# Graph aggregation as products of exact bfloat16 parts, with earlier gathers and a new order of attention's turns

## The chip, the core and the metric

One core of a Trainium2 chip runs the whole program: TensorE (PE in the profile; PEld is its weight loads), VectorE (DVE), ScalarE (ACT), GpSimd (POOL) and SyncE (SP, which only issues transfers). The engines run side by side and meet at semaphores. The metric is the device time of one execution in microseconds; before the change the median of three runs is 892.15 us (891.47 to 894.31).

## The reference, cut to what matters

`x` is 1250 rows of 512 float32 numbers; a graph of 20000 edges is given by `src` and `dst`. Two layers follow one another, each a graph step and a mixture of experts:

```python
x = x + _L0_gnn_ref(_layernorm(x), ..., edge_index, W)   # attention along the edges, 8 heads
x = x + _L0_ffn_ref(_layernorm(x)[None], ...)[0]         # 8 experts, the best 2 for each row
x = x + _L1_gnn_ref(_layernorm(x), W, b, gamma, beta, src, dst)
x = x + _L1_ffn_ref(...)                                  # 6 experts, the best 1
```

The third is the one whose arithmetic changes:

```python
h = x * rsqrt(deg_out)[:, None]
agg = segment_sum(h[src], dst)          # sum over incoming edges
h = agg * rsqrt(deg_in)[:, None]
h = layernorm(h @ W + b, gamma, beta)
return gelu(h)
```

The kernel makes `agg` as a dense product: (1250 x 1250 matrix of edge counts) times (1250 x 512 rows h).

## The kernel before

Rows are worked in T = 10 tiles of P = 125; the 512 features are C = 4 chunks of 128. Every engine has its program written out by hand, in order; each instruction waits in its engine's queue for the semaphores it names. There is no scheduler.

**Counts (0 to 178 us).** Edge lists become matrices of counts and of logarithms, stored to DRAM as `counts_d` and `logs_d` (float32), while PE also projects q, k and v. This runs inside a branch (`all_hold`), which the inputs here take; the other arm is for graphs of another kind.

**Attention (178 to 500 us).** 40 units u, four for each row tile, two heads each. In one unit PE does `scores(u+1)` for two thirds of the columns, `turn_output(u-2)` (L731, the turned output of an older unit), `turn_weights(u)` (L704, 20 transposes in 5 blocks of 4, each block moved out of PSUM by ACT, or by DVE for blocks 2 and 4), every fourth unit `turn_normed_row` (L749), then the last third of the scores (L693) and `weigh_values(u-1)` (L722). DVE subtracts logs and keeps minima (L1935), moves blocks (L1942), adds outputs to X. Beside it, tile by tile, runs the routing for the first experts: DVE finishes a tile's statistics in unit 5+4i, POOL makes its root (`rstd_tile`, L1512 and L1513), PE makes logits in unit 7+4i, DVE picks two experts, POOL makes the masks (`masks_of`, L1523), and PE ranks them in unit 8+4i (L766). POOL scatters rows into `slots0_d` by their ranks.

**First experts (500 to 649 us).** MT0 = 27 tiles of 128 slots go through three products (L802) with transposes between (L809), two norms and two GELUs, in a software pipeline. POOL makes two roots a tile (`inverse_rms`, L1573). DVE moves a tile's result to SBUF (`move_made`, L2147), SP stores it back to `slots0_d` (`store_rows0`, L440). Not all 27 tiles hold rows: the inputs here fill 24, and the others lie behind them.

**Gather and aggregate (649 to 736 us).** When every tile is stored, POOL gathers each row's two results (`gather_rows`, L1606, two indirect transfers a tile of rows), DVE adds them to X (`add_rows`, L2216), takes statistics (`row_stats`, L1741), POOL makes a root times the out-degree's (`row_root`), DVE scales the row (`rows_over_root`, L2223) into `HS[i]`, and PE multiplies `HS[i]` with the tile's counts (`aggregate`, L932): 2 pieces of 500 columns by 4 chunks, accumulated over the 10 tiles in all 8 PSUM banks. Gathers are issued AHEAD = 3 tiles ahead: gather i stands behind the root of tile i-2 in POOL's queue. While PE waits for the first rows it runs products whose result nobody reads (`keep_busy`, L924). The last 250 columns (`aggregate_rest`) need free banks and come later.

**Projection and second routing (736 to 818 us).** PE alternates `project` (L959), the four `aggregate_rest` and the routing products; DVE does bias, layer norm, GELU's input, best expert and slot of each tile; POOL scatters the tiles (L1654). **Second experts (818 to 891 us).** 15 tiles, the same way.

Of the kernel before, what the change touches and what calls it, by code (L numbers as in the profile page):

```python
# [8 lines left out]
I32 = mybir.dt.int32  # L9
# [28 lines left out]
FAR = 1.0e28  # L38
TM = 128
# [3 lines left out]
BUSY_AHEAD, BUSY_BETWEEN = 44, 12  # L43
E0, H0, K0 = 8, 256, 2
MT0 = (K0 * N + E0 * (TM - 1)) // TM
E1, H1 = 6, 256
# [48 lines left out]
def gnn_moe_kernel(nc, x, src, dst, L0_gnn_W, L0_ffn_gate_w, L0_ffn_w1, L0_ffn_w2, L0_ffn_w3,  # L95
                   L0_ffn_n1, L0_ffn_n2, L1_gnn_W, L1_gnn_b, L1_gnn_gamma, L1_gnn_beta,
                   L1_ffn_w_gating, L1_ffn_gamma, L1_ffn_w1, L1_ffn_w2, out):
    counts_d = nc.dram_tensor("counts_d", (N, N), F32).ap()
    logs_d = nc.dram_tensor("logs_d", (N, N), F32).ap()
# [3 lines left out]
    with ExitStack() as ctx:  # L103
# [51 lines left out]
        def ring(off, width, n):  # L155
# [12 lines left out]
        CS_C = R_B[0:P, 10000:10000 + (T - 2 * C) * N].rearrange("p (i n) -> p i n", i=T - 2 * C)  # L168
        counts_of = [part[:, i, :] for part, n in ((CS_A, C), (CS_B, C), (CS_C, T - 2 * C)) for i in range(n)]
        HS = [R_B[0:P, 12544 + D * i:12544 + D * i + D] for i in range(T)]  # L170
        BIAS, GAMMA, BETA = (R_B[:, 6144 + 512 * k:6656 + 512 * k] for k in range(3))
        AGT = R_A[:, 0:C * N].rearrange("p (c n) -> p c n", c=C)
        HG = [R_B[0:P, 18688 + D * k:18688 + D * k + D] for k in range(3)] + [R_B[0:P, 8192:8192 + D]]
# [6 lines left out]
        rows = [R_A[0:P, WIDE * n:WIDE * n + WIDE] if n < 12 else R_B[0:P, WIDE * (n - 12):WIDE * (n - 12) + WIDE]  # L180
                for n in range(K0 * T)]
# [3 lines left out]
        count_rows = [R_B[0:P, 14308 + N * k:14308 + N * k + N] for k in range(5)]  # L185
        ident = sb("ident", [128, 128])
# [39 lines left out]
        ssum = sb("ssum", [128, LANES])  # L226
        rms = sb("rms", [128, LANES])
# [6 lines left out]
        def small_bank(b, n):  # L234
# [23 lines left out]
        names = """x_in edges_in w_in wq_in wg_in consts zero_made zeros_out idx_step halves_made idx_turned  # L258
            span_step diag_made span_sums ctl_sums ctl_ready win_made hot slots_free gen_win gen_hot
            gen_free gen_step packed_out unpacked_out ct_made ln_made ln_masked ct_turned ct_moved  # L260
# [6 lines left out]
            y_made y_moved y_out0 y_out1 y_out2 counts_in0 counts_in1 counts_in2 logs_out0 logs_out1  # L267
            vec_in hs_made agg_made agt_moved hg_made hg_biased hg_stat hg_rstd hg_shift hg_gelu gate_sums
            xg_made w1b_in w2b_in gam_in log1_made g1_step g1_exp rank1_made deg_out_made log1_taken
            mask1_made slot1_ready rank1_taken token_made x_kept gate1_made slot1_made rows1_out  # L270
# [16 lines left out]
        y_out = [s["y_out0"], s["y_out1"], s["y_out2"]]  # L287
# [12 lines left out]
        def _(sp):  # L300
# [57 lines left out]
            def load_counts_of(tiles):  # L358
                for i in tiles:
                    if i > 4:  # L360
                        sp.wait_ge(S("deg_out_made"), i - 4)
                    move(count_rows[i % 5], counts_d[i * P:i * P + P, :], count_rows_in[i % 5])
            load_counts_of(range(5))
            for i in range(2, 5):
                load_logs(i)
            load_counts_of((5, 6))
            load_logs(5)
            load_counts_of((7, 8))
            load_logs(6)
            load_counts_of((9,))  # L370
            load_logs(7)
            load_logs(8)
            sp.wait_ge(S("deg_out_made"), T)
            for e in range(E0):
                sp.dma_start(W3E[:, e, :].rearrange("p (c n) -> p c n", c=2),
                             L0_ffn_w3[e].rearrange("(c p) n -> p c n", c=2)).then_inc(S("w3e_in"), 16)
# [51 lines left out]
            def load_counts(i):  # L428

                if i == 0:  # L430
# [2085 lines left out]
```

## Time and profile before

| | us |
|---|---|
| median of three runs | 892.15 |
| profiled execution, its own time | 892.8 |
| its span in the profile | 891.1 |
| PE busy | 839.9 |
| DVE busy | 556.9 |
| ACT busy | 374.2 |
| POOL busy | 207.2 |

The span is what the profile's clock covers; the time of the same execution is 1.7 us longer. A busy PE is not a PE at its peak: the ends of matmuls are modelled. The mean granted clock of TensorE is 0.984 of full speed. An engine's idle time costs only where another engine waits for it.

### The profile page before, as it was taken

What the parts mean: (1) busy time and instruction counts of PE and PEld (TensorE: products, weight loads), DVE (VectorE), ACT (ScalarE), POOL (GpSimd) and SP (SyncE); (2) the same over time, 40 slices, a digit from 0 to 9 for tenths busy, and PEclk for the clock granted to TensorE, in tenths of its full rate; (3) what the DMA queues carried; (4) which work ended last, traced back from release to release, by engine and by line L of the source; (5) the groups of instructions that cost most, each with busy time, mean ns of one, the idle gap of its engine ahead of it and who ended that gap; (6) DMA issues with size and microseconds to landing.
All of it is one profiled execution on the core that took longest, in us unless ns stands there. A gap on an engine that the chain in (4) does not pass through costs nothing.

```text
span 891.1 us, 16170 instructions
## 1 busy us (share of the span) xinstructions
PE 839.9 (94%) x5189; PEld 569.9 (64%) x5189; DVE 556.9 (62%) x1838; ACT 374.2 (42%) x680; POOL 207.2 (23%) x380
## 2 busy tenths in 40 slices
PE   5999999899999999999999899999979999996996
PEld 2456554367777777777777677777664445675664
DVE  6489999267778788778777265555533514875111
ACT  1234544366565566666566233334300012543331
POOL 4200000000022112201202332212245511465353
PEclk9999999999999999999999999999999999996999
DMA  9818888795111232110925546544136250175550
GB/s 261 324 29 220 220 209 210 171 322 137 31 49 57 57 101 61 44 39 25 306 78 156 200 115 212 160 155 154 48 95 138 69 189 12 36 258 136 155 170 22
DMA packets 87362, 121.00 MB, mean 136 GB/s; under 512 B 40781, under 2 KB 50157, under 8 KB 87021
## 3 DMA queue, kind: packets, MB, share of 16 engines
q1 hardware_dynamic: 73677, 101.82, 38.9%
q0 software_dynamic: 13600, 18.11, 7.3%
q8 instruction: 46, 0.75, 0.4%
q14 instruction: 39, 0.32, 0.1%
HBM read 65.52 MB, written 57.08 MB: 138 GB/s over the span
## 4 chain that ended last, share of the span: by engine, by line
PE 76%; DVE 11%; DMA 5%; issue 3%; ACT 2%; POOL 1%; SPq 1%; DVEq 0%; POOLq 0%; ACTq 0%
PE ps L802 18%; PE ps L693 11%; PE ps L722 10%; PE ps L932 10%; PE ps L704 8%; PE ps L583 5%; PE ps L959 4%; PE ps L809 4%; DVE R_B L1834 3%; PE ps L588 2%; DVE R_B L1833 2%; DMA R_A<-slots_d 1%; DVE R_A L1935 1%; PE ps L524 1%; PE ps L759 1%
## 5 line engine op out<-in xcount | busy, mean ns | idle before, releaser
L802 PE MATMUL ps<-R_B,R_A 128*128 x612 | 185.2, 445 | 1.7 <-ACT R_A L1302 0.6
L802 PEld LDWEIGHTS ps<-R_B,R_A 128*128 128x128 f32 x612 | 111.6, 193 | 34.6 <-issue 24.5
L1238 ACT ACTIVATE R_A<-R_A,neg_max 125x1250 f32<-125x1250 f32 x80 | 106.6, 1333 | 56.9 <-DVE neg_max L1935 56.9
L1935 DVE CUSTOM_DVE_ANT_0 R_A<-ps,R_B,neg_max 125x417 f32<-125x417 f32 (+1 forms) x160 | 97.6, 648 | 29.1 <-PE ps L693 29.1
L693 PE MATMUL ps<-R_B 64*125 64x417 f32 (+1 forms) x480 | 106.5, 544 | 1.9 <-ACT XN L1180 1.5
L722 PEld LDWEIGHTS ps<-R_W,XN 125*64 125x64 f32 x1600 | 85.3, 136 | 23.1 <-issue 23.0
L704 PE MATMUL ps<-ident,R_A 125*125 125x125 f32 x800 | 98.7, 278 | 0.0
L704 PEld LDWEIGHTS ps<-ident,R_A 125*125 125x125 f32 x800 | 94.9, 188 | 1.5 <-DVE R_W L1942 0.7
L722 PE MATMUL ps<-R_W,XN 125*64 125x125 f32 x1600 | 94.7, 272 | 0.0
L1245 ACT ACTIVATE R_W<-ps 125x500 f32<-125x500 f32 x120 | 66.1, 585 | 51.4 <-PE ps L704 51.4
L583 PE MATMUL ps<-XT,R_W 128*128 128x500 f32 (+1 forms) x192 | 72.5, 523 | 0.6 <-ACT XT L1163 0.6
L1935 DVE CUSTOM_DVE_ANT_0 R_A<-ps,R_B 125x417 f32<-125x417 f32 x80 | 44.1, 590 | 45.1 <-PE ps L693 32.4
L1834 DVE TENSOR_SCALAR R_B<-R_B 125x418 bf16<-125x418 uint16 x180 | 69.0, 383 | 0.0
L809 PEld LDWEIGHTS ps<-ident,R_A 128*128 128x128 f32 x306 | 38.3, 142 | 34.5 <-issue 20.0
L693 PEld LDWEIGHTS ps<-R_B 64*125 64x125 f32 x480 | 39.7, 183 | 29.4 <-issue 21.6
L809 PE MATMUL ps<-ident,R_A 128*128 128x128 f32 x306 | 49.5, 277 | 7.5 <-DMA R_A<-slots_d 4.0
L1942 DVE COPY R_W<-ps 125x500 f32<-125x500 f32 x80 | 53.7, 671 | 3.5 <-PE ps L704 3.4
L1573 POOL TENSOR_TENSOR rms<-ssum,half_pow 128x1 f32<-128x1 f32 x54 | 30.0, 557 | 102.0 <-DVE ssum L2115 67.5
L1833 DVE TENSOR_SCALAR R_B<-R_B 125x125 bf16<-125x125 uint16 x180 | 44.9, 249 | 13.5 <-PE ps L524 13.1
L583 PEld LDWEIGHTS ps<-XT,R_W 128*128 128x128 f32 x192 | 36.9, 195 | 25.4 <-issue 23.7
L524 PE MATMUL ps<-R_B 125*125 125x418 bf16 x180 | 43.5, 351 | 6.7 <-DVE R_B L1834 5.0
L1549 POOL IOTA R_B<- 125x4 int32 x2 | 0.3, 148 | 195.4 <-DVE mv L1742 195.4
(270 smaller groups left out, 1167.6 us busy)
## 6 DMA issues: line engine op xcount, KB each, us to landing
slots_d<-R_B SPq DMA_DIRECT2D x9, 2322.0 KB, 12.4
R_B<-in_L_ffn_w_dram SPq DMA_DIRECT2D x28, 512.0 KB, 6.8
R_A<-slots_d SPq DMA_DIRECT2D x27, 256.0 KB, 2.8
slots_d<-R_A SPq DMA_DIRECT2D x27, 256.0 KB, 2.4
counts_d<-R_A SPq DMA_DIRECT2D x10, 546.9 KB
logs_d<-R_B SPq DMA_DIRECT2D x10, 546.9 KB
R_B<-logs_d SPq DMA_DIRECT2D x10, 546.9 KB
R_B<-counts_d SPq DMA_DIRECT2D x10, 546.9 KB
```

The costliest lines, as they stand in the source:

```text
L583: ins = pe.matmul(b[:, 0:z - a], Wqkv[:, c, w:w + 128], XT[:, c, a:z], start=c == 0, stop=c == C - 1)
L693: pe.matmul(bank(2 * h + g % 2, P, z - a), QT[r:r + DH, i, j, :], KT[r:r + DH, j, a:z], start=True, stop=True).then_inc(S("s_made"), 1)
L704: ins = pe.transpose(bank(4 + n % 3, P, P, k * P), SC[u % 2][h][:, kt * P:kt * P + P], ident[0:P, 0:P])
L722: ins = pe.matmul(ps[r:r + DH, 512 * 7:512 * 7 + P], XN[:, kt, (2 * j + h) * DH:(2 * j + h) * DH + DH], PT[u % 2][:, T * h + kt, :], start ...
L802: ins = pe.matmul(bank(b, TM, width), lhs[:, c * TM:c * TM + TM], flat[:, bass.ds(e * (n * width) + c * width, width)], start=c == 0, stop ...
L809: ins = pe.transpose(bank(b, 128, TM, c * TM), source[:, c * 128:c * 128 + 128], ident[:, :])
L932: return pe.matmul(bank(b, 128, z - a), HS[i][:, c * 128:c * 128 + 128], counts_of[i][:, a:z], start=i == 0, stop=i == T - 1)
L1238: act.activation(SC[u % 2][h], SC[u % 2][h], ACT.Exp, bias=neg_max[:, 2 * (u % 2) + h:2 * (u % 2) + h + 1], scale=-1.0, accum_out=den[:, 2 ...
L1245: act.activation(PT[u % 2][:, 4 * b:4 * b + 4, :], bank(4 + ring_at(u, b) % 3, P, 4 * P).rearrange("p (i n) -> p i n", n=P), ACT.Copy).the ...
L1833: dve.tensor_scalar(oh_dst[:, slot, :], iota_dst, win[:, 0, w:w + 1], None, ALU.is_equal)
L1834: return dve.tensor_scalar(hot_of[:, slot, 0:width], iota_src[:, 0:width], win[:, 1, w:w + 1], win[:, 2, w:w + 1], ALU.is_equal, ALU.mult)
L1935: dve.tensor_tensor_reduce(SC[u % 2][h][:, a:z], bank(2 * h + g % 2, P, z - a), LNB[i % 2][:, a:z], -1.0, least if t else 3.0e38, ALU.add, ...
```

## The change

**Aggregation.** A float32 product is replaced by three bfloat16 products: a row is split into three bfloat16 parts whose sum is the row (first part; what it leaves; what both leave), and the counts are split into a low and a high plane of bfloat16 (the high one a multiple of 256). In the arm that the inputs take, counts are small and only the low plane is multiplied. ACT makes parts one and two, DVE the subtractions and part three. POOL makes the planes during attention, and SP stores them to a new DRAM matrix `planes_d`, from which the aggregation's operand is loaded in place of `counts_d`. The planes of tiles 8 and 9 are loaded during the experts (`LOW_C`), where before their counts were loaded while rows were gathered.

```diff
+ROUNDER = 1.5 * 2.0 ** 31
+PARTS = 3
-BUSY_AHEAD, BUSY_BETWEEN = 44, 12
+BUSY_AHEAD, BUSY_GATHERED, BUSY_BETWEEN = 6, 18, 12
...
-            def aggregate(i, c, n, b):
+                def aggregate(i, k, c, n, b):
...
-                return pe.matmul(bank(b, 128, z - a), HS[i][:, c * 128:c * 128 + 128], counts_of[i][:, a:z],
-                                 start=i == 0, stop=i == T - 1)
+                    for plane in planes:
+                        ins = pe.matmul(bank(b, 128, z - a), HP[i][k][:, c * 128:c * 128 + 128], (low_of, high_of)[plane][i][:, a:z],
...
-                pe.wait_ge(S("hs_made"), i + 1)
+                    for k, made in enumerate((S("hs_first"), S("hs_second"), S("hs_third"))):
+                        pe.wait_ge(made, i + 1)
...
+            def first_part(i):
+                act.wait_ge(S("hs_made"), i + 1)
+                act.activation(HP[i][0], HS[i % 3], ACT.Copy).then_inc(S("hs_first"), 1)
+            def second_part(i):
+                act.wait_ge(S("hs_left"), i + 1)
+                act.activation(HP[i][1], HS[i % 3], ACT.Copy).then_inc(S("hs_second"), 1)
...
+            def left_of_first(i):
+                dve.wait_ge(S("hs_first"), i + 1)
+                dve.tensor_tensor(HS[i % 3], HS[i % 3], HP[i][0], ALU.subtract).then_inc(S("hs_left"), 1)
+            def third_part(i):
+                dve.wait_ge(S("hs_second"), i + 1)
+                dve.tensor_tensor(HP[i][2], HS[i % 3], HP[i][1], ALU.subtract).then_inc(S("hs_third"), 1)
...
-                row_stats(X, i)
                 if i:
                     rows_over_root(i - 1)
+                row_stats(X, i)
+                if i > 1:
+                    third_part(i - 2)
+                if i:
+                    left_of_first(i - 1)
...
+            def split_counts(i):
+                pool.wait_ge(count_rows_in[i % 5], 32 * (i // 5) + 48)
+                above_zero(pool, S("planes_out"), 32 * (i - 1))
...
+                link(pool.tensor_scalar(row, count_rows[i % 5], -127.5, ROUNDER, ALU.add, ALU.add))
+                link(pool.tensor_scalar(high, row, ROUNDER, None, ALU.subtract))
+                pool.tensor_tensor(low, count_rows[i % 5], high, ALU.subtract).then_inc(S("planes_made"), 1)
             for i in range(T - 1):
                 rstd_tile(S("ln_stat"), T + i + 1, i, 1.0, S("ln_rstd"))
+                if i < T // 2:
+                    split_counts(2 * i)
+                    split_counts(2 * i + 1)
```

SP's queue takes the stores of planes between its loads of logs and counts (`store_planes`), each behind `planes_made`. On PE, everything from attention on is now written inside both arms of the branch (`attention_and_after((0,))` in the one taken); its order is the same but for what follows.

**The gathers' wait.** POOL waited for all 27 stored tiles; it now waits for the first product of the last tile (the first 8 buffers of rows lie where the first weights were) and for as many stores as tiles hold rows. The stores are now in one chain (`y_stored`), each issued when the one before has landed. The wait for all tiles comes ahead of gather 4, and a gather now stands ahead of a root.

```diff
+                if t == 12:
+                    pool.wait_ge(S("gate_step"), 1)
+                    stored = pool.value_load(used_i[0:1, 0:1], min_val=16 * LEAST_TILES, max_val=16 * MT0)
...
-            for k in range(LANES):
-                pool.wait_ge(y_out[k], 16 * (MT0 // LANES))
-            pool.wait_ge(S("y_made"), MT0)
+            pool.wait_ge(S("h1_made"), MT0)
+            pool.wait_ge(S("y_stored"), stored)
+            pool.tensor_tensor(rms[:, 2:3], half_pow[:, 0:1], half_pow[:, 0:1], ALU.mult)
...
             for i in range(AHEAD, T):
+                if i == EARLY_GATHERS:
+                    pool.wait_ge(S("y_made"), MT0)
+                    pool.wait_ge(S("y_stored"), 16 * MT0)
+                gather_rows(i)
                 row_root(i - AHEAD + 1)
-                gather_rows(i)
```

Since the parts lie in other memory, the numbering of three tiles (`number_rows(range(7, T))`) on POOL now waits for the whole aggregation, and the gates of the two experts are made on DVE just ahead of the last `move_made`.

**Attention's order.** PE turns the old output behind the third block of weights in place of ahead of the first; DVE moves block 2 ahead of adding the output.

On PE, one plain attention unit (`ps` PSUM, `R_A` the scores, `R_W` weights and outputs). Before:

```order
L693 MATMUL ps<-R_B 125x417 x4
L731 MATMUL ps<-ident,R_W 125x128
L704 MATMUL ps<-ident,R_A 125x125 x20
L693 MATMUL ps<-R_B 125x416 x2
L722 MATMUL ps<-R_W,XN 64x125 x20
```

Now:

```order
L690 MATMUL ps<-R_B 125x417 x4
L701 MATMUL ps<-ident,R_A 125x125 x12
L728 MATMUL ps<-ident,R_W 125x128
L701 MATMUL ps<-ident,R_A 125x125 x8
L690 MATMUL ps<-R_B 125x416 x2
L719 MATMUL ps<-R_W,XN 64x125 x20
```

The output's turn moved behind 12 of the 20 transposes; nothing was added.

On POOL, the end of the first experts and the gathers (`rms` the last roots, `rstd` the roots of gathered rows). Before:

```order
L1573 TENSOR_TENSOR rms<-ssum,half_pow 128x1 x50
L1606 DMA R_A<-slots_d,slot 125x516 x6
L1512 TENSOR_SCALAR rstd<-mv,out_max 125x1
L1513 TENSOR_TENSOR rstd<-rstd,half_pow 125x1
L1512 TENSOR_SCALAR rstd<-mv,out_max 125x1
L1513 TENSOR_TENSOR rstd<-rstd,half_pow 125x1
L1606 DMA R_A<-slots_d,slot 125x516 x2
```

Now:

```order
L1641 TENSOR_TENSOR rms<-ssum,half_pow 128x1 x31
L1672 TENSOR_TENSOR rms<-half_pow 128x1
L1677 DMA R_B<-slots_d,slot 125x516 x6
L1567 TENSOR_SCALAR rstd<-mv,out_max 125x1
L1568 TENSOR_TENSOR rstd<-rstd,half_pow 125x1
L1677 DMA R_B<-slots_d,slot 125x516 x2
L1567 TENSOR_SCALAR rstd<-mv,out_max 125x1
L1568 TENSOR_TENSOR rstd<-rstd,half_pow 125x1
L1677 DMA R_A<-slots_d,slot 125x516 x2
```

Gather 3 now stands behind one root, not two, and so does each gather after it: one tile more is under way.

On DVE, what one tile of gathered rows takes (`R_W` the scaled row, `R_B` its parts). Before:

```order
L2216 SCALAR_TENSOR_TENSOR X<-R_A,gates,X 125x512 x2
L1741 BN_STATS stats<-X 125x6
L1742 BN_AGGR mv<-stats 125x2
L2223 TENSOR_SCALAR R_B<-X,mv,rstd 125x512
```

Now:

```order
L2299 SCALAR_TENSOR_TENSOR X<-R_B,gates,X 125x512 x2
L2306 TENSOR_SCALAR R_W<-X,mv,rstd 125x512
L1820 BN_STATS stats<-X 125x6
L1821 BN_AGGR mv<-stats 125x2
L2316 TENSOR_TENSOR R_B<-R_W,R_B 125x512
L2311 TENSOR_TENSOR R_W<-R_W,R_B 125x512
```

Two subtractions of 125x512 are added to a tile, and the scaling of the tile before moved ahead of the statistics.

## Rows read from the trace of the kernel before

**Rows 1.** Page: the chain that ended last, shares of the span by engine
```profile
PE 76%; DVE 11%; DMA 5%; issue 3%; ACT 2%; POOL 1%; SPq 1%; DVEq 0%; POOLq 0%; ACTq 0%
```

**Rows 2.** Stretches: busy us of each engine (instructions), PEclk, DMA share, GB/s
```profile
300.00:400.00 100.00, 99.52 (x984) 76.10 (x984) 81.51 (x266) 60.93 (x106) 15.86 (x40) 1.00 0.23 65
...
660.00:680.00 20.00, 16.68 (x60) 9.24 (x59) 10.78 (x20) 0.00 (x0) 11.88 (x15) 0.91 0.35 98
...
760.00:780.00 20.00, 20.00 (x92) 14.66 (x91) 17.11 (x42) 11.74 (x15) 10.29 (x19) 1.00 0.13 40
```

**Rows 3.** Chain that ended last, 40 to 765 us: start, duration, what
```profile
49.23 1.61 PE ps L524 x9
...
666.93 69.04 PE ps L932 x160
...
746.27 4.22 PE ps L932 x20
```

**Rows 4.** Timeline 640 to 735, POOL: start, duration, instruction, idle before
```profile
644.49 0.55 POOL L1573 TENSOR_TENSOR rms<-ssum,half_pow 128x1 f32<-128x1 f32 x1 [3.45 <-DVE ssum L2129]
653.22 1.30 POOL L1606 DMA_INDIRECT R_A<-slots_d,slot  x1 [8.19 <-issue]
...
660.89 1.48 POOL L1606 DMA_INDIRECT R_A<-slots_d,slot  x1 [0.30 <-issue]
...
666.55 1.03 POOL L1512 TENSOR_SCALAR rstd<-mv,out_max 125x1 f32<-125x1 f32 x1 [2.50 <-DVE mv L1742]
...
671.79 0.27 POOL L1512 TENSOR_SCALAR rstd<-mv,out_max 125x1 f32<-125x1 f32 x1
```

**Rows 5.** Timeline 640 to 735, DVE
```profile
649.19 0.69 DVE L2147 COPY R_A<-ps 128x512 f32<-128x512 f32 x1 [2.47 <-PE ps L802]
...
660.54 1.54 DVE L2216 SCALAR_TENSOR_TENSOR X<-R_A,gates,X 125x512 f32<-125x512 f32 x2 [8.88 <-DMA R_A<-slots_d,slot]
...
666.36 0.52 DVE L2223 TENSOR_SCALAR R_B<-X,mv,rstd 125x512 f32<-125x512 f32 x1
...
676.02 1.54 DVE L2216 SCALAR_TENSOR_TENSOR X<-R_A,gates,X 125x512 f32<-125x512 f32 x2 [6.32 <-DMA R_A<-slots_d,slot]
...
692.22 1.54 DVE L2216 SCALAR_TENSOR_TENSOR X<-R_A,gates,X 125x512 f32<-125x512 f32 x2 [9.29 <-DMA R_A<-slots_d,slot]
...
715.15 1.54 DVE L2216 SCALAR_TENSOR_TENSOR X<-R_B,gates,X 125x512 f32<-125x512 f32 x2 [3.90 <-DMA R_B<-slots_d,slot]
```

**Rows 6.** Timeline 640 to 735, SP, PE and ACT
```profile
679.98 0.85 SPq L325 DMA_DIRECT2D R_B<-counts_d  x2
...
650.85 12.75 PE L924 MATMUL ps<-ones,ident 128*128 128x128 f32 x112
666.93 28.80 PE L932 MATMUL ps<-XT,R_B 125*128 125x500 f32 x64 [3.33 <-DVE R_B L2223]
...
730.14 0.59 ACT L1360 ACTIVATE R_A<-ps 128x500 f32<-128x500 f32 x1 [81.58 <-PE ps L932]
```

**Rows 7.** Groups by line and shape: busy, mean ns, idle before
```profile
L1741 DVE BATCH_NORM_STATS2 stats<-X 125x6 f32<-125x512 f32 x30 | 20.7, 689 | 0.8
...
L2277 DVE TENSOR_TENSOR X<-X,R_B 125x512 f32<-125x512 f32 x10 | 6.8, 680 | 0.4 <-ACT R_B L1365 0.3
...
L1532 POOL TENSOR_TENSOR work<-R_A,counted 125x8 f32<-125x8 f32 x20 | 3.6, 200 | 26.5 <-DVE counted L1992 26.5
...
L1644 POOL TENSOR_TENSOR R_B<-ones,before 125x125 bf16<-125x125 f32 x1 | 0.4, 446 | 0.0
```

**Rows 8.** Attention: PE's waits 200 to 490; timelines 380 to 405
```profile
PE ps L749 <- DVE R_W L1942: 2.1, 9, 0.8
...
380.77 0.57 POOL L1513 TENSOR_TENSOR rstd<-rstd,half_pow 125x1 f32<-125x1 f32 x1
399.80 0.60 POOL L1523 TENSOR_SCALAR R_A<-iota,R_B 125x8 f32<-125x8 f32 x2 [18.45 <-DVE R_B L1984]
...
401.13 0.39 PE L766 MATMUL ps<-counted,before 126*126 126x8 f32 x2
```

More of the change, by code:

```diff
@@ L178, in gnn_moe_kernel @@
         W2B = R_B[:, 12544:18688].rearrange("p (e n) -> p e n", e=E1)
-        rows = [R_A[0:P, WIDE * n:WIDE * n + WIDE] if n < 12 else R_B[0:P, WIDE * (n - 12):WIDE * (n - 12) + WIDE]
-                for n in range(K0 * T)]
+        EARLY_GATHERS = 4
+        rows = [R_B[0:P, WIDE * n:WIDE * n + WIDE] if n < K0 * EARLY_GATHERS else
+                R_A[0:P, WIDE * (n - K0 * EARLY_GATHERS):WIDE * (n - K0 * EARLY_GATHERS) + WIDE] for n in range(K0 * T)]
         scaled = [R_W[0:P, WIDE * i:WIDE * i + WIDE] for i in range(7)] +\
@@ L665, in _ @@
                     project(n)
+                attention_and_after((0, 1))
             pe.end_ifs()
[L668 to L682 removed]
@@ L795, in _ @@
-            pe.wait_ge(S("slot_made"), 1)
-            expert = {}
-            def product(b, lhs, weights, e, n, width):
-                flat = weights.rearrange("p e n -> p (e n)")
-                for c in range(n):
-                    ins = pe.matmul(bank(b, TM, width), lhs[:, c * TM:c * TM + TM],
-                                    flat[:, bass.ds(e * (n * width) + c * width, width)],
-                                    start=c == 0, stop=c == n - 1)
-                return ins
-            def turn_chunks(b, source, n):
-                for c in range(n):
-                    ins = pe.transpose(bank(b, 128, TM, c * TM), source[:, c * 128:c * 128 + 128], ident[:, :])
-                return ins
@@ L1638, in logit_roots, with number_rows @@
                 pool.tensor_tensor(out_max[:, :], out_max[:, :], half_pow[0:P, :], ALU.pow).then_inc(S("ln_rstd"), 1)
-            for i in range(T):
-                ins = pool.iota(scaled[i][:, D:WIDE].bitcast(I32), [[0, WIDE - D]], base=P * i, channel_multiplier=1)
-            link(ins)
+            def number_rows(tiles):
+                for i in tiles:
+                    ins = pool.iota(scaled[i][:, D:WIDE].bitcast(I32), [[0, WIDE - D]], base=P * i, channel_multiplier=1)
+                link(ins)
+            number_rows(range(0, 7))
             pool.tensor_copy(before_b, before[0:P, 0:P])
@@ L1670, in _ @@
             unit_root(5)
+            pool.wait_ge(S("agg_made"), C * len(AGGREGATED))
+            number_rows(range(7, T))
             scatter_unit(0)
```

892 lines of the change are left out of this document (476 added, 416 removed).

## The prediction

> **What bounds the kernel now.** I read the chain's shares first: PE holds 76% of the span [rows 1]. So a stretch gets shorter only where PE's own work shrinks or where PE waits. The busy time by stretches then says where it waits. In attention PE is busy 99.52 of 100 us, DVE 81.51 [rows 2]: only PE's instructions count there. From 760 to 780 PE is full again, but DVE has 17.11 of 20 us, so there what PE gives up DVE may keep. The aggregation of the first 1000 columns stands in the chain as one piece of 69.04 us from 666.93 on, 160 records, two for each of 80 float32 products [rows 3]; the last 250 columns are four pieces of 4.22 us. Ahead of 666.93 the chain lies elsewhere: the last expert tile is moved at 649.19 [rows 5], POOL waits 8.19 us and issues the first gather at 653.22 [rows 4], its rows reach DVE at 660.54, the first scaled row is made at 666.36 [rows 5], and PE, whose unread products fill 650.85 to 663.6, sits 3.33 us idle [rows 6]. So two things are for sale: some 17 us between the last tile and the first product, and 86 us of products.
>
> **The change part by part.** Times are those of the profiled execution (892.8 us, of which the span is 891.1), 0.65 above the median of the runs.
>
> *Start of the gathers.* POOL now needs the last root of the experts, made 644.49 to 645.04 [rows 4], the first product of the last tile, and the stores of the 24 tiles that hold rows. The last of those is three tiles ahead of the one moved at 649.19, and tiles come at least 3 us apart, so its store has landed before 645. The root ends last. Behind it come the added small operation (0.55 us, like that root) and the issue's gap of 0.3: first gather at 646.0 in place of 653.22, 7.2 us earlier. Six issues of about 1.5 us and one root stand as before between this and the second tile, so I carry the 7.2 us on: DVE adds tile 0 at 653.3, tile 1 at about 656.7. The scaling now comes ahead of the statistics (0.9 us sooner), and a copy on ACT (0.6 us, as its 500-wide moves take 0.59 [rows 6], plus a semaphore) is added: first product at 659.6, that is 7.2 us earlier. Bounds: 0 if the stores came last after all, 8.2 us if the whole wait went. The wait for all tiles ahead of gather 4 is met at about 652.5 (the last move and a store), when POOL is still issuing gather 1 or 2; it hides there.
>
> *The products.* Nine bfloat16 products of 418 columns took 1.61 us back to back [rows 3], 0.428 ns a column; 500 columns are 0.214 us. Three in place of one float32 product (69.04 / 80 = 0.863) are 0.642. 240 of them: 51.4 us. No row shows a 500-column bfloat16 product with 128 weight columns; if its weights were not hidden it would lose, at most to 0.863 / 3 = 0.288 and no gain; I take 0.214, since the 418-column row changes its weights each time too.
>
> *Do the parts come fast enough?* On DVE a tile now takes two additions 1.54 and a scaling 0.52 [rows 5], statistics 0.69 [rows 7] and 0.18 behind them, and two subtractions, which I price like the addition of two 512-wide rows, 0.68 each [rows 7]: 4.3 us, against 24 products = 5.14 us on PE. POOL has two issues of 1.5 and a root of about 0.9: 3.9 us. ACT has 1.2 us. All are below PE. What is late is the beginning: part three of tile 0 stands behind tile 2's additions, tile 1's scaling and tile 2's statistics, about 664.2, while parts one and two keep PE busy from 659.6 to 663.0. PE loses 1.2 us there and then runs through: 664.2 + 1.7 + 9 x 5.14 = 712.2. The supply before came at (715.15 - 676.02) / 6 = 6.5 us a tile [rows 5]; its worst gap, tile 5 at 692.22 after 9.29 us idle, follows the transfer of counts that SP issued at 679.98 [rows 6], and that load now stands among the experts' tiles, while the high plane comes after the last row. Even at 6.5 us a tile the last part would be ready at about 712, so 6.3 us is the pace from which the supply decides. Aggregation then takes 52.6 in place of 69.0: 16.4 us less, and with the start PE is through at 712.2 in place of 736.0.
>
> *Handing over.* The eight banks used to close 0.86 us apart, and ACT (0.59 a move, first at 730.14 [rows 6]) was ahead of PE. Now they close 0.21 apart in the last 1.7 us, and the projection needs four moved: four moves of 0.56 from 710.9 on end at 713.1. Cost 1.0 us.
>
> *The last columns.* 40 products of 0.422 (4.22 / 10) become 120 of 0.107: 4.0 us of PE. DVE is nearly full in that stretch, 17.11 of 20 us [rows 2], so I let 3 through; bounds 0 and 4. The numbering that waits for the aggregation stands just ahead of the first scatter, a few tenths of iota that fit in POOL's wait for the first slot.
>
> *Attention.* PE's turned rows waited for DVE's move of block 2: nine times, 2.1 us in total [rows 8]. That move now comes 0.39 us earlier (two 64-wide additions), more than the 0.23 it lacked, so up to 2.1 us go. Against it: two additions and the logits behind them come later in each unit, and the rank product at 401.13 follows the mask (0.60 and 0.29 us from 399.80) by only 0.44 us [rows 8]. The planes are put on POOL between the root, through at 381.34, and the mask at 399.80 after 18.45 us idle [rows 8]: six operations of 125x1250. The nearest rows are a two-input operation of 125 elements, 446 ns, and one of 8, 200 ns [rows 7]: 2.1 ns an element, 2.8 us for 1250. At that for all six it is 16.8 us, inside the 18.9 us that there are; with one-input ones nearer half of it, about 11. Upper bound 4.46 each, ten times the short row. The added 2 x 0.6 MB a tile of transfers fall in a stretch with a DMA share of 0.23 [rows 2]. I take 1 us gained, between -2.1 and a loss that the rivals price.
>
> *The experts.* A store waits for the one before (landing in 2.4 us in the median by the page's list of transfers, less than a tile of the pipeline), the planes have the bytes of the counts, the gates' exponential fits in ACT's idle time: nothing, hidden by the pipeline's slack. At worst one late tile of rows, 1 to 2 us.
>
> Sum: 7.2 + 16.4 - 1.0 + 3.0 + 1.0 = 26.6 us. 892.8 - 26.6 = 866.2; as a median 0.65 less: **866 us**.
>
> **Rivals.**
> *A, masks come late (slower than before).* Place: POOL in attention's units 5 to 22. If the six operations take 4.46 us each, 26.8 us stand in a room of 18.9, PE's rank product waits 7.9 us in each of five tiles, 39 us: 905 us. It begins to cost at 3.2 us an operation and makes the kernel slower than before at 4.0. For it: no row has a POOL operation this long. Against: the two short rows give 2.8. 6%.
> *B, POOL and DVE hold each other up.* A root's first operation took 1.03 us while DVE was about to add rows and 0.27 us when DVE was idle [rows 4]. If it also goes the other way, some seven units of attention have a plane operation of 2.8 us in front of one of DVE's small ones; DVE has 18.5% of about 8 us, 1.5 us, in hand, so up to 1.3 us x 7 = 9 us reach PE: 870 in the middle, 875 at the end. 12%. The Trainium skill ("SBUF — State Buffer", section "Who interferes with whom") says that a VectorE instruction with two SBUF inputs and a GpSimd one that reads SBUF exclude each other, the second waiting for all of the first; by that rule B happens, and the 1.03 beside 0.27 agrees with it in one direction.
> *C, the clock.* After 3.33 us idle the granted clock was 0.91 of full over 660 to 680 [rows 2], and the first 64 records took 28.80 us [rows 6], where 64 at 27.0 would follow from 0.42 a record: 1.8 us lost. PE now idles about 2.2 us ahead of 659.6 and 1.2 at 663. At worst both first tiles run at 1.2 GHz, 10.3 us of work in double time less the waits: 9 us. The middle is 869 us. 12%.
> *D, no earlier start.* Something else holds the first rows, or the early transfers are slow beside the last stores: up to 7.2 us back, 873 us. 7%.
> *E, the supply runs out.* At 7.5 us a tile in place of 6.3, 9 x 1.2 = 11 us: 877. For it: gathers landed over 9 us late once. Against: what went with that has moved. 6%.
> The forecast has 57%, with its own range 861 to 871.
>
> **How the numbers follow.** The low end adds what I held back: 1 us of the last columns, 1.1 of attention, 1.2 at the first parts, and an unknown few in the tail where everything comes sooner: 857. The high end takes in B, C and D and leaves A and half of E out: 877. A measurement tells 0.3%, 2.7 us, from no change. Only A, or several rivals together, end there: faster 0.93, same 0.02, slower 0.05.
>
> **What would show it.** Right: first gather near 646, first aggregation product near 660, PE then without a wait of over 0.3 us from 665 to 712, bfloat16 products 0.214 apart, the projection near 713, the rank products of attention without a wait, PE's wait for block 2 gone. Wrong: plane operations over 3 us, a wait of PE's rank product for POOL's mask, units longer than 7.4 us beside them (A, B); a clock under 0.9 between 655 and 680 (C); the first gather at 650 or later (D); PE waiting for part three in late tiles (E); or a tail from the projection to the end that isn't 3 us shorter than its 155 us.

## The result and the profile after

The changed kernel takes 882.61 us in the median of four runs (881.59 to 883.54); the kernel before, beside it on the same chip, 892.94 us in four. The ratio is 0.9884, 95% interval 0.9862 to 0.9907: 10 us faster, where I had forecast 26 and a range of 857 to 877 us. The profiled execution has a span of 880.1 us.

Five moments, each the first or last start of a line in the trace (for the exponential, of the readout behind it), say where the 16 us went (us from the span's start):

| | before | after | moved by |
|---|---|---|---|
| last exponential of attention | 488.0 | 501.9 | +13.9 |
| first gather | 653.2 | 660.1 | +6.9 |
| first aggregation product | 666.9 | 673.9 | +7.0 |
| first projection product | 735.8 | 727.3 | -8.5 |
| end of the span | 891.1 | 880.1 | -11.0 |

So attention, where I had put 1 us of gain, lost some 14 us, and everything behind it gained 24.9 (403.1 us from the last exponential to the end before, 378.2 after), where my terms made 25.6.

Attention first. One stretch of it in the profile of the changed kernel, against [rows 2] (us, then busy us and instructions of PE, PE's weight loads, DVE, ACT, POOL, then PE's granted clock, DMA share, GB/s), and two short stretches of it:
```profile
300.00:400.00 100.00, 92.42 (x893) 70.42 (x895) 90.86 (x245) 54.42 (x95) 72.11 (x56) 0.97 0.34 98
```
```profile
232.00:236.00 4.00, 4.00 (x32) 2.49 (x33) 3.86 (x8) 1.14 (x2) 3.83 (x3) 0.62 0.12 33
236.00:240.00 4.00, 4.00 (x42) 2.91 (x39) 2.41 (x8) 2.47 (x5) 3.92 (x2) 1.00 0.42 130
```
PE is busy 92.42 of 100 us in place of 99.52, for 91 instructions fewer. DVE is busier by 9 us though it does less. That is the sign to look for: an engine whose busy time grows without more instructions is being held up. The granted clock over 232 to 236 is 0.62, part of it at the lower level of 1.2 GHz, right behind an idle time of PE.

PE's waits in attention (for whom, us in total, times, the longest), against the 2.1 us of [rows 8]:
```profile
PE ps L746 <- DVE R_W L2021: 12.9, 5, 2.8
PE ps L763 <- POOL counted L1580: 2.5, 2, 1.3
```
POOL's timeline, 224 to 247 us (start, duration, line, operation, shapes, idle before):
```profile
224.18 4.49 POOL L1619 TENSOR_SCALAR R_B<-R_B 125x1250 f32<-125x1250 f32 x1
228.75 3.45 POOL L1620 TENSOR_SCALAR R_B<-R_B 125x1250 bf16<-125x1250 f32 x1
232.28 2.55 POOL L1621 TENSOR_TENSOR R_B<-R_B 125x1250 bf16<-125x1250 f32 x1
...
245.48 0.60 POOL L1578 TENSOR_SCALAR R_A<-iota,R_B 125x8 f32<-125x8 f32 x2
```
DVE's, in the same stretch:
```profile
224.75 4.20 DVE L2050 TENSOR_SCALAR R_B<-X,mv,rstd 125x512 f32<-125x512 f32 x1
...
232.38 2.46 DVE L2032 SCALAR_TENSOR_TENSOR rden<-neg_max,rden 125x2 f32<-125x2 f32 x1
...
259.96 3.87 DVE L2050 TENSOR_SCALAR R_W<-X,mv,rstd 125x512 f32<-125x512 f32 x1
```
PE's:
```profile
231.75 1.09 PE L746 MATMUL ps<-ident,R_B 125*128 125x125 f32 x4 [2.84 <-DVE R_W L2021]
232.78 1.75 PE L690 MATMUL ps<-R_B 64*125 64x416 f32 x4
...
242.00 0.97 PE L690 MATMUL ps<-R_B 64*125 64x416 f32 x4
```
Three things are to be seen. POOL's scalar operations of 1250 columns take 4.49 and 3.45 us and the subtraction 2.55, not 2.8 each; with the second tile they fill 21.2 us up to the mask. DVE's normed row (L2050) takes 4.20 us, 0.54 when POOL is still: it starts at 224.75 and ends at 228.95, with POOL's L1619, which ends at 228.67. And DVE's move of block 2, queued a little behind, comes late, so PE's turn of the normed row waits 2.84 us; its next products (L690) then take 1.75 us in place of 0.97.

Then the part that came as worked out. POOL at the end of the experts' tiles, against [rows 4]:
```profile
659.12 0.55 POOL L1641 TENSOR_TENSOR rms<-ssum,half_pow 128x1 f32<-128x1 f32 x1 [3.46 <-DVE ssum L2208]
659.63 0.19 POOL L1672 TENSOR_TENSOR rms<-half_pow 128x1 f32<-128x1 f32 x1
660.07 1.38 POOL L1677 DMA_INDIRECT R_B<-slots_d,slot  x1 [0.25 <-issue]
```
PE over the aggregation, against [rows 3, 6]:
```profile
673.87 3.55 PE L931 MATMUL ps<-XT,R_B 125*128 125x500 bf16 x16 [1.84 <-ACT R_B L1397]
678.78 17.27 PE L931 MATMUL ps<-XT,R_B 125*128 125x500 bf16 x80 [1.36 <-DVE R_B L2316]
695.89 20.50 PE L931 MATMUL ps<-XN,R_B 125*128 125x500 bf16 x96
716.23 10.31 PE L931 MATMUL ps<-R_B 125*128 125x500 bf16 x48
727.27 7.96 PE L962 MATMUL ps<-R_W,R_A 128*125 128x512 f32 x18 [0.73 <-ACT R_A L1414]
```
and the stretch from 675 to 695 us:
```profile
675.00:695.00 20.00, 18.64 (x88) 8.17 (x87) 16.19 (x30) 5.17 (x9) 17.25 (x18) 1.00 0.40 108
```
The gather follows the last root by 0.95 us with no wait for stores; before it came 8.7 us behind its root [rows 4]. The 240 products run from 673.87 to 726.5, 0.2135 us each (20.50 / 96), with one wait of 1.36 us for part three.

### The profile page after: what moved, and what is told of

Same layout as the page of the kernel before. It is cut to its first block, busy times and chain, and to the rows that moved or that the text cites. A ratio compares the mean times of both kernels' runs of the same rounds, so it can differ in the third digit from the quotient of the medians.

```text
span 880.1 us, 16436 instructions
## 1 busy us (share of the span) xinstructions
PE 813.0 (92%) x5245; PEld 551.6 (63%) x5245; DVE 603.7 (69%) x1859; ACT 385.7 (44%) x700; POOL 318.4 (36%) x411
## 4 chain that ended last, share of the span: by engine, by line
PE 73%; DVE 12%; issue 5%; DMA 4%; POOL 3%; ACT 2%; SPq 0%; DVEq 0%; POOLq 0%; ACTq 0%
PE ps L800 18%; PE ps L690 10%; PE ps L719 9%; PE ps L701 9%; PE ps L931 7%; PE ps L614 5%; PE ps L619 4%; PE ps L807 4%; PE ps L962 3%; DVE R_B L1913 3%; DVE R_B L1912 2%; DVE R_A L2014 2%; PE ps L555 1%; DMA slots_d<-R_B,slot 1%; DMA R_A<-slots_d 1%
## 5 line engine op out<-in xcount | busy, mean ns | idle before, releaser
L690 PE MATMUL ps<-R_B 64*125 64x417 f32 (+1 forms) x480 | 107.9, 550 | 1.5 <-ACT XN L1220 1.5
L719 PEld LDWEIGHTS ps<-R_W,XN 125*64 125x64 f32 x1600 | 88.0, 139 | 24.8 <-issue 24.8
L701 PE MATMUL ps<-ident,R_A 125*125 125x125 f32 x800 | 102.3, 277 | 0.0
L719 PE MATMUL ps<-R_W,XN 125*64 125x125 f32 x1600 | 97.5, 277 | 0.5 <-DVE X L2042 0.5
L690 PEld LDWEIGHTS ps<-R_B 64*125 64x125 f32 x480 | 40.2, 185 | 28.7 <-issue 20.8
```

The source lines that it names most:

```text
L690: pe.matmul(bank(2 * h + g % 2, P, z - a), QT[r:r + DH, i, j, :], KT[r:r + DH, j, a:z], start=True, stop=True).then_inc(S("s_made"), 1)
L701: ins = pe.transpose(bank(4 + n % 3, P, P, k * P), SC[u % 2][h][:, kt * P:kt * P + P], ident[0:P, 0:P])
L719: ins = pe.matmul(ps[r:r + DH, 512 * 7:512 * 7 + P], XN[:, kt, (2 * j + h) * DH:(2 * j + h) * DH + DH], PT[u % 2][:, T * h + kt, :], start ...
```

## The experiments

The kernels below ran in four groups, each group on a chip of its own beside the kernel before: e1 to e4 (the kernel before takes 896.9 us there in the median), e5 to e8 (897.5), e9 to e12 (899.5), e13 to e15 (897.2). So the ratio to the kernel before is what is compared, above all between groups. The changed kernel's own ratio in the second group is 0.9887 (e5), as it was beside the result (0.9884).

| run | ratio to before | interval | last exponential, us | span, us |
|---|---|---|---|---|
| e5 changed kernel | 0.9887 | 0.9852 to 0.9922 | 508.4 | 884.9 |
| e1 planes of 8 columns | 0.9641 | 0.9594 to 0.9687 | 487.7 | 863.6 |
| e2 planes behind the row | 1.0058 | 1.0034 to 1.0082 | 519.4 | 901.4 |
| e3 before, new order | 0.9949 | 0.9922 to 0.9976 | 487.6 | 890.6 |
| e4 low plane on ACT | 0.9626 | 0.9574 to 0.9679 | 486.6 | 864.7 |
| e6 scalar operations only | 0.988 | 0.9813 to 0.9947 | 506.8 | 885.7 |
| e7 subtraction only | 0.9653 | 0.9606 to 0.9701 | 487.6 | 865.0 |
| e8 two operations | 0.9891 | 0.9843 to 0.994 | 506.2 | 885.2 |
| e9 two, behind the row | 0.9691 | 0.9647 to 0.9734 | 487.9 | 866.5 |
| e10 two, first in 625 + 625 | 0.9621 | 0.9575 to 0.9666 | 487.9 | 862.5 |
| e11 as e4, old wait | 0.9707 | 0.9665 to 0.9748 | 488.7 | 874.6 |
| e12 as e4, old order | 0.9715 | 0.9668 to 0.9762 | 492.0 | 871.4 |
| e13 two, 626 + 624 | 0.966 | 0.9624 to 0.9696 | 486.7 | 865.6 |
| e14 two, 1249 + 1 | 0.9889 | 0.9841 to 0.9937 | 507.6 | 886.4 |
| e15 three, scalar ones halved | 1.005 | 1.0033 to 1.0067 | 522.0 | 900.8 |

The intervals of two ratios overlap where they are less than some 0.9% apart; the last exponential tells attention's part to a microsecond or two.

**e1: is it POOL's plane operations?**
```diff
-link(pool.tensor_scalar(row, count_rows[i % 5], -127.5, ROUNDER, ALU.add, ALU.add))
+if i < 2:
+    link(pool.memset(row, 0.0))
+link(pool.tensor_scalar(row[:, 0:8], count_rows[i % 5][:, 0:8], -127.5, ROUNDER, ALU.add, ALU.add))
... (the other two operations to 8 columns likewise)
```


> The changed kernel with POOL's three plane operations a tile cut from 1250 to 8 columns (the low plane is left out but for 8 columns; two buffers are zeroed once); stores and loads of planes, the new order of turns and all the rest stay. Theory P (POOL's plane operations cost all that attention lost, 14.6 us and the 1 us that the new order brings): 882.6 - 15.6 = 867 us, and PE busy 99 of 100 us in attention. Rival O (the new order of turns, or the planes' transfers, cost it): no more than 2 us gained, 881 to 883. Half and half would be 874.


Ratio 0.9641, PE busy 100.00 of 100 us over 300 to 400, and no wait of PE for DVE or POOL from 200 to 430. All the loss of attention is the work of these operations; transfers and order cost nothing. First gather 645.7, first aggregation product 659.3, projection 712.3 us: 646.0, 659.6 and 713.1 were forecast. The 867 us that I expected are 0.971 of the 892.9 they were reckoned from, so e1 came 0.7% lower, some 6 us; 4 to 5 us of it are what the new order gives above the 1 us that I had (e3).

**e2: the hold of the row or late masks?**
```diff
 if i < T // 2:
+    pool.wait_ge(S("xn_made"), T + i + 1)
     split_counts(2 * i)
```


> The changed kernel, but POOL starts the planes of a stretch only when DVE has made the normed row (five more waits of about 1.2 us). Theory B (POOL's long operations hold DVE's normed row, 3.1 to 3.9 us in place of 0.54 five times): the row takes 0.54 again; 5 x 3.3 = 16 us of DVE come back, of which DVE's slack of some 1.5 us a unit had hidden half, less 1.2 us of later masks each: 875 to 879 us. Rival A (it is the masks, late by what POOL's 21 us exceed its room of 18.9): 5 x 1.2 = 6 us more, 888 us.


Both missed: 1.0058, 15 us slower than the changed kernel. The row takes 0.54 us again and the wait for block 2 is gone, but PE's rank product now waits for POOL's mask:
```profile
PE ps L763 <- POOL counted L1580: 25.8, 5, 5.3
```
In the changed kernel the hold of 3.3 us had delayed PE and with it the moment at which the mask was due; so one loss hid the other. From the waits follows the room: at the first tile the mask's operations started 22.4 us behind the root (228.06 to 250.47) and PE waited 5.14 us, so about 17.3 us were to be had; at the other four 22.7 to 22.9 us and 5.1 to 5.3, so 17.6. I had 18.9, read in the old order of turns [rows 8]. The new order itself takes 1.2 us of that: with nothing long on POOL, the rank product starts 19.78 us behind the root in the kernel before and 18.56 us in e3.

**e3, e12: the order of attention's turns alone.**
```diff
-if 2 <= u:
-    turn_output(u - 2)
-turn_weights(u)
+turn_weights(u, range(0, 3))
+if 2 <= u:
+    turn_output(u - 2)
+turn_weights(u, range(3, BLOCKS))
... (on DVE the move of block 2 ahead of the output's addition)
```


> The kernel before with attention's new order of turns alone (the output's turn behind block 3 of the weights on PE, DVE's move of block 2 ahead of the output's addition). Theory P: PE's wait of 2.1 us in nine places goes, 891 to 892 us against 892.9. Rival O: this order is what costs the 14.6 us, 900 us or more.

> The kernel with the low plane on ACT and attention's old order of turns. By my term (1 us gained by the new order) 1 us slower; by the order-alone run's profile (last exponential 0.4 us sooner) 0.4; by that run's ratio (0.9949) 4 us. Looked at: the last exponential's start, 486.6 us with the new order.


0.9949 with the order alone, and 0.9715 against 0.9626 when it is taken back in e4: a gain of 4.6 us by the one, 8 by the other, both with wide intervals. The traces give it exactly. The rank product of eight tiles, all instructions of its line with their number, ns (least, median, most) and first and last start, in the old order (e12) and the new (e4):
```profile
L763 PE MATMUL ps<-counted,before x16: 254/265/275, 247.8 to 468.1; 126*126 126x8 f32 x16
```
```profile
L763 PE MATMUL ps<-counted,before x16: 254/264/276, 247.8 to 463.3; 126*126 126x8 f32 x16
```
28 units take 220.3 us in the old order and 215.5 in the new. A plain unit of PE shrinks, as these two pieces of the PE timeline show, of e12 and of e4:
```profile
286.86 0.37 PE L728 MATMUL ps<-ident,R_W 128*125 128x128 f32 x1
287.06 2.46 PE L701 MATMUL ps<-ident,R_A 125*125 125x125 f32 x20
289.45 0.97 PE L690 MATMUL ps<-R_B 64*125 64x416 f32 x4
```
```profile
255.35 1.57 PE L701 MATMUL ps<-ident,R_A 125*125 125x125 f32 x12
256.76 0.28 PE L728 MATMUL ps<-ident,R_W 128*125 128x128 f32 x1
256.87 1.03 PE L701 MATMUL ps<-ident,R_A 125*125 125x125 f32 x8
257.84 0.97 PE L690 MATMUL ps<-R_B 64*125 64x416 f32 x4
```
From the first turn to L690 2.59 us in the old order, 2.49 in the new. With the wait in front of the normed row that is 4.8 us in 28 units, 5 to 6 over the loop (last exponential 492.0 against 486.6). I had counted the wait alone. What makes the output's turn 0.1 us cheaper between two turns of weights no run shows.

**e4: the low plane on ACT.**
```diff
 for b in ACT_BLOCKS:
     move_block(u, b)
+if u % 2 and 7 <= u < 7 + 2 * T:
+    low_plane((u - 7) // 2)   # one act.activation(low, count_rows[i % 5], ACT.Copy)
```


> The changed kernel with the low plane made on ACT by one copy of 1250 float32 to bfloat16 per tile, behind the move of block 3, in ten odd units from 7 on; POOL only zeroes two buffers once. The high plane is left out, which this branch (counts below 256) does not read. ACT is idle 1.47 us there in the kernel before and an exponential of 1250 takes 1.34, so the copy fits by 0.1: theory P says 867 to 869 us. Rival (ACT's exponentials come late behind the copy, 1.0 us in each of ten units): 877 us.


0.9626: the rival (877 us, a ratio of 0.982) is out, and the kernel is 0.8 to 1.0% below theory P, whose 867 to 869 us are ratios of 0.971 to 0.973; about half of that is again the new order's larger gain, and the interval is 0.5% to either side. The copy stands in ACT's gap (ACT timeline):
```profile
257.51 0.59 ACT L1285 ACTIVATE R_W<-ps 125x500 f32<-125x500 f32 x1 [0.36 <-PE ps L701]
257.99 1.24 ACT L1311 ACTIVATE R_A<-R_B 125x1250 bf16<-125x1250 f32 x1
259.97 1.34 ACT L1278 ACTIVATE R_A<-R_A,neg_max 125x1250 f32<-125x1250 f32 x1 [0.74 <-DVE neg_max L2023]
```

**e5 to e8: which operation, and is it the hold alone?**
```diff
 e6: -pool.tensor_tensor(low, count_rows[i % 5], high, ALU.subtract)...
     +pool.tensor_tensor(low[:, 0:8], count_rows[i % 5][:, 0:8], high[:, 0:8], ALU.subtract)...
 e7: the two tensor_scalar left out; the plane's buffers zeroed once
 e8: -link(pool.tensor_scalar(row, count_rows[i % 5], -127.5, ROUNDER, ALU.add, ALU.add))
     -link(pool.tensor_scalar(high, row, ROUNDER, None, ALU.subtract))
     +link(pool.tensor_scalar(high, count_rows[i % 5], ROUNDER, ROUNDER, ALU.add, ALU.subtract))
```


> The changed kernel once more, beside the next three on one chip. Both theories: its ratio to the kernel before as on the first chip, 0.986 to 0.991.

> The changed kernel with the subtraction that makes the low plane cut to 8 columns (so the low plane is left out but for them); POOL keeps the two one-input operations a tile, 4.5 and 3.4 us: 16.4 us in place of 21 between root and mask. With the planes held back behind the normed row the masks came 5.3 us late after 22.5 us, so 16.4 is in time. Theory B (the normed row is held by the first operation, 3 to 4 us): that hold stays, five waits of PE for block 2 of 2.6 us stay, 2.5 us of mask waits go: ratio 2 us below the changed kernel's, 880 of 882.6. Theory A (late masks): all 15 us come back, 867.

> The changed kernel with POOL's subtraction alone (counts less a high plane zeroed once, so the low plane is right for these inputs and the high plane is left out): one two-input operation of 2.5 us a tile. Theory B: the normed row now falls into 2.5 us of which 0.6 to 1.2 are over when it comes, so it is held 1.3 to 1.9 us, which DVE's slack hides: 867 to 869. Rival F (each long POOL operation costs DVE the same, whatever its length): a third of the loss stays, 872.

> The changed kernel with the rounding in one POOL operation (x + R - R, right for counts up to 128), then the subtraction: 6 us a tile, 12 in all, masks in time. The first operation in the normed row's way is 3.4 us in place of 4.5. Theory B: the row is held about 2.4 us less what is over, 1 us less than now; so some 1.5 of the 2.6 us waits stay in each of five units, and the masks' 2.5 us go: 872 to 876. Theory A: 867.


e6 keeps the loss (0.988; block 2 waited for 12.8 us in five places, no wait for a mask): the hold alone is enough, and late masks added next to nothing on top. e7 loses next to nothing (0.9653): the row takes 1.7 to 1.85 us at four tiles, and DVE has nearly all of that in hand (PE's waits for block 2 are 2.2 us in all, 0.6 at most). e8 missed its number: the fused operation takes 4.5 us, as long as the one it replaces, so the row is held 3.9 us as before and the ratio stays (0.9891), though POOL is done 6 us early. POOL's price goes by the scalar steps in an operation: 4.5 us with two, 3.4 with one, and 2.4 to 2.6 for two tensors and no scalar.

**e9: both ways out at once.** e8 with the wait of e2.
```diff
 (in e8)
 if i < T // 2:
+    pool.wait_ge(S("xn_made"), T + i + 1)
     split_counts(2 * i)
```


> Two operations a tile (4.5 and 2.6 us, as measured), started only when DVE has made the normed row. POOL needs 1.3 + 14.2 + 0.5 = 16 us from root to mask, under the 17.2 us that the run with three operations behind the row allows. Theory B+A (the row's hold is the loss, and lateness begins at 17.2): both are avoided, ratio to before 0.963 to 0.970, normed rows of 0.54 us, no wait of PE for a mask. Rival (what DVE does later in those 15 us, its two-entry product and its cast, is held as dearly): 0.975 or more.


0.9691, and normed rows of 0.54 us: both losses are avoided. PE still waits for five masks, 2.6 us in all, 0.7 at most; at the first tile the mask's operations begin 17.75 us behind the root (228.20 to 245.95) and PE waits 0.49 us, so again some 17.3 us were to be had. What holds them is no longer POOL's own work but DVE's pick, for which POOL waits 2.40 us; a little ahead of the pick DVE's product of two columns takes 1.44 us beside POOL's subtraction, in place of 0.16. That no mask would be waited for was expected, and missed by these 2.6 us.

**e10, e13, e14: what decides whether the row is held?**
```diff
-link(pool.tensor_scalar(high, count_rows[i % 5], ROUNDER, ROUNDER, ALU.add, ALU.subtract))
+for a, z in ((0, 625), (625, 1250)):      # e13: 626 + 624, e14: 1249 + 1
+    ins = pool.tensor_scalar(high[:, a:z], count_rows[i % 5][:, a:z], ROUNDER, ROUNDER, ...)
+link(ins)
```


> Two operations a tile with the first cut into two halves of 625 columns, 2.3 us each, no wait for the row. Theory B (DVE is held to the end of the one POOL operation that runs): the normed row takes 2.2 instead of 3.9 us, PE's five waits shrink from 2.6 to about 1 us: ratio to before 0.974 to 0.980. Rival Q (POOL keeps the way over operations issued back to back): 3.9 us or more and 0.989 as now.

> Two operations a tile, the first cut into 626 and 624 columns. Parity (an even number of elements takes the way that DVE's normed row needs, an odd one doesn't): the row is held to the end of the half or of both, 2.2 or 3.9 us, ratio to before 0.975 to 0.989. Length (only an operation of well over 625 columns holds): 0.54 us as with 625, ratio 0.962.

> Two operations a tile, the first cut into 1249 columns and 1. Parity: the row takes 0.54 us though POOL's operation is 4.5 us long, ratio 0.962. Length: held 3.9 us, ratio 0.989.


I expected a shorter hold and saw none. POOL and DVE in e10:
```profile
230.99 4.66 POOL L1621 TENSOR_SCALAR R_B<-R_B 125x625 bf16<-125x625 f32 x2
```
```profile
231.55 0.54 DVE L2052 TENSOR_SCALAR R_B<-X,mv,rstd 125x512 f32<-125x512 f32 x1
```
and in e14:
```profile
262.70 4.88 POOL L1621 TENSOR_SCALAR R_B<-R_B 125x1249 bf16<-125x1249 f32 x2
```
```profile
263.59 3.90 DVE L2052 TENSOR_SCALAR R_W<-X,mv,rstd 125x512 f32<-125x512 f32 x1
```
POOL is busy with the same work, 4.66 us against 4.88, and the row meets it 0.56 and 0.89 us after its start. With halves, odd or even (e13: 0.54 us too), no hold shows; with 1249 columns the row is held. So length decides, not parity, and my rule "held to the end of what runs" is wrong for operations of 625 columns. Length here means columns and not time. In e4 POOL zeroes two buffers of 1250 columns, each in half the time of a 625-column operation, and the row beside them waits for both (POOL's and DVE's timelines of e4):
```profile
229.01 1.15 POOL L1634 MEMSET R_B<- 125x1250 f32 x1
230.09 1.15 POOL L1635 MEMSET R_A<- 125x1250 f32 x1
229.71 1.81 DVE L2059 TENSOR_SCALAR R_B<-X,mv,rstd 125x512 f32<-125x512 f32 x1
```
Another instruction of DVE, the product of two columns, hints at a reason, though no run shows that it is the row's. Beside a half of 625 columns that starts at 244.09 us in e15 it is held too, but only to 0.7 us after that start:
```profile
244.31 0.50 DVE L2035 SCALAR_TENSOR_TENSOR rden<-neg_max,rden 125x2 f32<-125x2 f32 x1
```
The normed rows of e10 came 0.56 to 0.89 us after the start of a half, near the end of such a hold or behind it. Where between 626 and 1249 columns the change lies, why POOL lets go so early, and whether a row that met the first half microsecond of a short operation would be held, stays open. e10 is the fastest kernel of all, 0.9621, level with e4 (0.9626) within the intervals. Both beat the kernel before by 3.7% and the changed one by 2.6%. e8 to e10, e13 and e14 round counts above 128 up into the high plane, which this branch doesn't read, so they hold for smaller counts only; e4 holds for all counts of this branch.

**e15: late masks with no hold of the row.** The changed kernel's three operations, the two scalar ones in halves.
```diff
-link(pool.tensor_scalar(row, count_rows[i % 5], -127.5, ROUNDER, ALU.add, ALU.add))
+for a in (0, 625):
+    ins = pool.tensor_scalar(row[:, a:a + 625], count_rows[i % 5][:, a:a + 625], -127.5, ROUNDER, ALU.add, ALU.add)
+link(ins)
... (the second likewise, linked at each half)
```


> The changed kernel, all three operations, the two one-input ones each in two parts of 625 columns: the same work of POOL, 21.5 to 22 us from root to mask. If halves of 625 leave the row alone here too, the masks are late by what exceeds 17.2 us: 4.5 us in five tiles, 22 us and some clock: ratio to before 0.988 to 0.995, no better than the changed kernel (0.9887), now as a wait of PE for POOL's mask of 4 to 5 us, five times. Rival (the masks cost only the 2.5 us seen in the changed kernel): 0.965 to 0.970.


The mechanism came as written, five waits:
```profile
PE ps L763 <- POOL counted L1580: 23.6, 5, 5.0
```
The price was higher, 1.005. The stretch from 300 to 400 us of e15 shows the rest:
```profile
300.00:400.00 100.00, 90.17 (x851) 69.01 (x847) 73.20 (x233) 54.22 (x93) 73.27 (x58) 0.93 0.31 92
```
PE waits 5 us a tile and is then granted 0.93 of its clock on average, against 0.97 in the changed kernel and 1.00 in e10. So the changed kernel was within reach of being slower than the one before: the hold that cost it 2.6 us a tile spared it the 5.

**e11: the gathers' wait.** e4 with the old wait ahead of the first gather.
```diff
-pool.wait_ge(S("y_stored"), stored)
+pool.wait_ge(S("y_made"), MT0)
+pool.wait_ge(S("y_stored"), 16 * MT0)
```


> The kernel with the low plane on ACT, but the gathers wait for all tiles and all stores again ahead of the first. My sum's first term: 7.2 us later at the first gather and at the end, ratio to before 0.971 where the one without it gave 0.9626. Rival D (the earlier start is given back before the products): no difference.


0.9707, the 0.971 expected, against 0.9626, 7.3 us (with intervals of 4 us to either side); the first gather comes 168.4 us behind the last exponential in place of 159.8, after this wait:
```profile
656.16 0.19 POOL L1682 TENSOR_TENSOR rms<-half_pow 128x1 f32<-128x1 f32 x1 [7.59 <-DMA slots_d<-R_A]
657.05 1.30 POOL L1687 DMA_INDIRECT R_B<-slots_d,slot  x1 [0.69 <-issue]
```

## Why the prediction was wrong

**Start of the gathers, -7.2.** Right: 7.8 by the traces (from the last root to the first gather, 8.73 us before and 0.95 after), 7.3 by e11.

**The products, -16.4 with a wait for part three of 1.2.** Right: 52.7 us against my 52.6, the wait 1.36. The supply never ran out, and the clock from 655 to 695 us was granted in full (1.00, where it had been 0.91 over 660 to 680 [rows 2]). Rivals C, D and E did not happen.

**Handing over and last columns, +1.0 and -3.0.** Right: the projection starts 0.73 us after an idle PE, and from it to the end are 152.8 us in place of 155.3, 2.5 less.

**Attention, -1 between -2.1 and the rivals' losses.** Wrong, in two terms of opposite sign. The new order gives 5 to 6 us, not 1 (e3, e12). And the planes on POOL cost 19 to 20 us in place of nothing: 12.9 + 2.5 us of waits, and the rest the lower clock behind them (0.62 over 232 to 236 us, where two groups of products take 1.75 and 2.64 us in place of 0.97 and 2.37, about 1 us a tile). From first to last exponential attention took 307.5 us before; with the new order and no loss it would be some 5.3 less, 302.2; it took 321.9. The kernels without this loss gain more than my 26.6: 32 to 34 us (e1, e4), mostly because the new order gives more than 1.

The step that failed reads: "I take 1 us gained", from "2.8 us for 1250" for each plane operation, "inside the 18.9 us that there are". Each half of it was mis-sized. Operations of 8 and 125 columns were scaled with two points, both two-input; the one-input ones, which I put at about half, are the dear ones, 4.49 and 3.45 us. The room was read in the old order of turns [rows 8]; in the new one it is 17.3 to 17.6 us, because the change that I priced beside it brings the rank product 1.2 us nearer to the root. With both right, the 21.2 us stand some 4 us above the room, and rival A, with 6%, would have been my main case; e15 shows it at 1.005, with waits of 4.6 to 5.0 us for its 22.2 us up to the mask.

What decided was rival B, which I had at 12% and 870 to 875 us. Its mechanism is shown, its place and price were not: I put it on "some seven units" and small operations and hid most of it in DVE's slack. It is one operation in each of five tiles, the normed row, held 3.3 us, of which PE sees 2.6, plus clock: 882.6. The trace had the one hint that I cited, a root of 1.03 us beside 0.27 [rows 4], which is the other direction. The Trainium skill ("SBUF — State Buffer", section "Who interferes with whom") also says that a VectorE tensor_scalar from SBUF can enter a two-port mode and then excludes GpSimd for the whole instruction, the first issued having the way. I used only its sentence on two inputs; the row's 4.20 us beside 0.54 agrees with that other one. "For the whole instruction" isn't borne out by e10, e13 and e15: a POOL operation of 625 columns ran on and the row took 0.54 us. The measurement decides. The sentence on two inputs, which I did use, came true as well, for DVE's product of two columns, but that hold is not what cost the time: in e6 no product was held, and the loss stayed.

That rivals A and B are tied, each hiding the other, I hadn't seen at all; it is why e2 came out slower and why the sum of the two waits in the profile after (15.4 us) could not be split by reading.

## What to carry to other kernels

When work is put on an idle engine, ask which instruction of the busy neighbours it stands beside, not only whether it fits the idle time; a DVE operation that takes 0.54 us can take 4.2 beside a long one on POOL, and cutting POOL's into halves was worth 24 us here (ratios of e8 and e10; their spans, on two chips, are 22.7 us apart) at no cost seen. Room for a late result is read in the kernel as it will be: another part of the same change may bring its reader nearer, here by 1.2 us. And before a wait is taken away that seems the whole loss, look at what was due at the same time: behind the wait of 2.8 us stood one of 5.3.

## What the runs showed of the hardware

- POOL, 125x1250 float32 in: 4.5 us with two scalar steps whatever the output's type (float32 or bfloat16), 3.4 with one, 2.4 to 2.6 for the subtraction of two tensors, 1.15 for zeroing. The two-input form is the cheapest but for that.
- DVE's one-input scaling of 512 float32 columns took 3.86 to 4.22 us beside a POOL operation of 1249 or 1250 columns with scalars, up to 1.85 beside a subtraction (e7), 1.81 beside two zeroings (e4), and 0.54 beside an operation of 625 or 626 columns.
- DVE's product of 2 columns with two inputs (L2032) took 2.46 us beside POOL's two-input subtraction, where it takes 0.16 alone. The one-input operations hold it too, but let it go before their own records end. In the changed kernel it ended 0.40 us ahead of L1620:
```profile
274.38 3.40 POOL L1620 TENSOR_SCALAR R_A<-R_A 125x1250 bf16<-125x1250 f32 x1
275.86 1.52 DVE L2032 SCALAR_TENSOR_TENSOR rden<-neg_max,rden 125x2 f32<-125x2 f32 x1
```
  In e2, e8 and e14, beside operations with two scalar steps, it took 1.6 to 3.1 us and ended some 0.6 us ahead of them; products that began within those last 0.4 or 0.6 us took 0.16. This fits the Trainium skill's rule ("SBUF — State Buffer", section "Who interferes with whom") that a VectorE instruction with two SBUF inputs contends with a GpSimd one that reads SBUF. That the hold lasts for the whole instruction fits the subtraction, and not these operations nor those of 625 columns (0.7 us in e15).
- ACT's copy of 125x1250 float32 to bfloat16 takes 1.24 us (e4).
